# Second feed-forward product from rounded high and low parts, and the normed tile written in two halves

## The reference, cut to what matters

```python
a  = softmax over l of (x x^T), times x                   # self-attention, 2 x 2048 x 128
b  = weighted values (correlation, small ODE step, proj)  # one later stage
ffn = 2 layers, each:
    h = shift_token(x);  q, k, v = split(h @ wqkv)        # 8 heads of 64
    q = l2norm(q) * qs;  k = l2norm(k) * ksc
    q, k = q*cos*s + rotate_half(q)*sin*s, k*cos/s + rotate_half(k)*sin/s
    x = x + local_attention(8*q, k, v) @ wo               # windows of 64, own and past
    h = layernorm(shift_token(x)) * lg + lb
    a, g = split(h @ w1 + b1)                             # 2 x 341 columns
    x = x + (a * gelu(g)) @ w2 + b2
```

## Time and profile before

| what | value |
|---|---|
| median of three runs | 1556.6 us |
| the profiled execution | 1558.34 us |
| its span, first to last instruction | 1556.5 us |
| mean granted TensorE clock | 0.978 |
| PE, weight loads | 1438.8 us (92%), 1118.7 us (72%) |
| DVE, ACT, POOL | 1290.2 (83%), 1237.4 (79%), 895.0 us (57%) |

### The profile page before, as it was taken

One profiled execution on the slowest core, in us unless ns is written; L12 is line 12 of the kernel. 1 busy time (PEld: TensorE's weight loads), 2 busy tenths in 40 slices (PEclk: granted clock), 3 DMA queues, 4 the chain that ended last, 5 costly groups with the idle time before them and its releaser, 6 DMA issues.

```text
span 1556.5 us, 46462 instructions
## 1 busy us (share of the span) xinstructions
PE 1438.8 (92%) x18975; PEld 1118.7 (72%) x18975; DVE 1290.2 (83%) x1692; ACT 1237.4 (79%) x1834; POOL 895.0 (57%) x626
## 2 busy tenths in 40 slices
PE   5999997899999999999998757899999999999998
PEld 3777874777777777777776554677777777777776
DVE  6778758888899888988985866889899998988984
ACT  4886867688888888888885757788888888888884
POOL 4333105576666666776762545676666666666761
PEclk9999999999999999999999878999999999999999
DMA  4312003576676666757550003666667566675562
GB/s 115 112 51 85 18 5 75 121 131 120 121 129 127 118 122 127 125 119 127 115 107 18 0 5 69 134 126 120 121 129 125 118 126 124 124 124 121 115 111 67
DMA packets 359855, 157.46 MB, mean 101 GB/s; under 512 B 299410, under 2 KB 335836, under 8 KB 359644
## 3 DMA queue, kind: packets, MB, share of 16 engines
q1 hardware_dynamic: 359644, 154.51, 49.7%
HBM read 27.29 MB, written 6.29 MB: 22 GB/s over the span
## 4 chain that ended last, share of the span: by engine, by line
PE 58%; DVE 20%; issue 6%; ACT 5%; SPq 5%; DMA 4%; POOL 2%; DVEq 0%; POOLq 0%; ACTq 0%
PE PS L199 8%; PE PS L201 7%; PE PS L200 7%; PE PS L852 6%; PE PS L914 5%; PE PS L871 5%; DMA t<-t 3%; PE PS L827 3%; PE PS L834 3%; DVE t L1276 3%; DVE t L1283 2%; DVE t L1259 2%; DVE t L1266 2%; PE PS L860 2%; SPq L706 2%
## 5 line engine op out<-in xcount | busy, mean ns | idle before, releaser
L1444 POOL TENSOR_TENSOR t<-t 128x512 f32<-128x512 f32 x256 | 321.1, 1275 | 189.7 <-DVE t L1276 189.4
L1438 POOL TENSOR_TENSOR t<-t 128x1024 f32<-128x1024 f32 x128 | 309.0, 2414 | 164.5 <-DVE t L1266 164.4
L1276 DVE TENSOR_TENSOR t<-t 128x1024 f32<-128x1024 f32 x128 | 206.9, 1617 | 0.1
L199 PE MATMUL PS<-wqh,HH 128*128 128x512 f32 x384 | 178.0, 464 | 15.8 <-DVE t L1266 9.5
L1259 DVE TENSOR_REDUCE t<-t 128x16 f32<-128x1024 f32 x128 | 154.7, 1209 | 31.4 <-ACT t L1059 31.4
L1295 DVE TENSOR_REDUCE t<-PS 128x8 bf16<-128x1024 f32 x128 | 156.1, 1219 | 20.4 <-PE PS L801 20.4
L1059 ACT ACTIVATE t<-PS 128x1024 f32<-128x1024 f32 x128 | 131.6, 1028 | 49.2 <-PE PS L201 49.1
L1283 DVE TENSOR_TENSOR t<-t,PS 128x1024 bf16<-128x1024 f32 x128 | 155.1, 1212 | 7.9 <-ACT PS L1079 7.7
L1093 ACT ACTIVATE t<-PS 128x1024 f32<-128x1024 f32 x128 | 131.6, 1028 | 36.0 <-PE PS L834 32.4
L1072 ACT CAST t<-t 128x1024 bf16<-128x1024 f32 x128 | 133.8, 1046 | 27.6 <-POOL t L1444 26.9
L1266 DVE SCALAR_TENSOR_TENSOR t<-t,PS 128x1024 f32<-128x1024 f32 x128 | 154.9, 1210 | 0.6 <-ACT t L1066 0.6
(11 more groups left out here) (242 smaller groups left out, 3400.9 us busy)
## 6 DMA issues: line engine op xcount, KB each, us to landing
t<-t SPq DMA_DIRECT2D x254, 130.0 KB, 2.4
t<-turns SPq DMA_DIRECT2D x128, 128.0 KB, 2.9
t<-yT SPq DMA_DIRECT2D x108, 128.0 KB
t<-t SPq DMA_TRANSPOSE x304, 3.4
t<-in_c_rope SPq DMA_DIRECT2D x32, 128.0 KB, 2.2
turns<-t SPq DMA_DIRECT2D x32, 128.0 KB, 2.1
t<-in_L_attn_a_x SPq DMA_DIRECT2D x4, 512.0 KB, 7.1
t<-yT SPq DMA_DIRECT2D x16, 127.8 KB
```

Source lines behind the costliest of these rows:

```text
L199: e.matmul(o, ah, bh, start=not more, stop=False, skip_group_check=True)
L1276: e.e.tensor_tensor(BL.ta[i % 2].rearrange("p (x h) d -> p x h d", x=2), BL.qn.rearrange("p (x h) d -> p x h d", x=2), cos.to_broadcast([1 ...
L1438: e.e.tensor_tensor(BL.tc.rearrange("p (x h) d -> p x h d", x=2), BL.qn.rearrange("p (x h) d -> p x h d", x=2), sin.to_broadcast([128, 2, ...
L1444: e.e.tensor_tensor(tv[:, :, 32 * s:32 * s + 32], tv[:, :, 32 * s:32 * s + 32], BL.tc[:, :, 32 * (1 - s):32 * (1 - s) + 32], ALU.add).then ...
```

## The change

What it does, in three parts:

1. `w2` is kept as `w2h` and `w2l` (fp32r). Its six DMAs move from the end of SP's load to the middle of self-attention, into the buffer `BS.stage`; ACT makes the high parts at t = 18 and 22 of self-attention, POOL the low parts behind `scale_turns(1)`.
2. The hidden chunk is split as well: ACT casts (`high_hidden`) and POOL subtracts (`low_hidden`), one of the three parts in each of the steps r = 14, 15 and 16. `second` runs nine fp32r matmuls (`halves`) on these instead of three fp32 ones. `BL.hf` has two buffers instead of three, and `gated` now waits for `ff_lo` (the low part is made) instead of `ff_m2`. Behind the last step the parts are made on ACT, POOL and, for the last two half chunks, DVE.
3. DVE's `normed` is two instructions (q, then k) with a semaphore each (`la_q0`, `la_qn`); PE's `project` waits for either half by itself; POOL's sine product is two instructions too, and POOL's `rope` is split into `sine` and `turned_sums`, with `low_hidden` between them.

```diff
         def product(p, i):
+            if p == NC - 2 and i == 2:
+                return BL.o.rearrange("p b h d -> p (b h d)")[0:CW[i], :]
             if p < NC - 1:
-                return BL.hf[i][0:CW[i], :]
+                return BL.hf[(p + i) % 2][0:CW[i], :]
...
+        def hidden(t, p, i):
+            if p < NC - 1:
+                return t[0:CW[i], 1, i * CH:(i + 1) * CH]
+            return t[0:CW[i], i // 2, (1, 3, 3)[i] * CH:((1, 3, 3)[i] + 1) * CH][:, cols(p)]
...
-                e.wait_ge(S.la_qn, hi(i))
-                for x in range(2):
+                for x, read in enumerate((S.la_q0, S.la_qn)):
+                    e.wait_ge(read, hi(i))
                     xs = slice(x * 512, (x + 1) * 512)
                     mm = halves(e.e, PS[:, x, :], h, hl, wqh[:, l, xs], wql[:, l, xs])
...
             def second(C, bank):
                 l = layer_of(C)
-                e.wait_ge(S.ld_w2, 16 * 6)
+                e.wait_ge(S.w_2l, 2)
                 for i in range(3):
-                    e.wait_ge(S.ff_hf, 3 * (NP * u + C) + i + 1)
-                    mm = e.e.matmul(PS[:, bank, wide(C)], w2[0:CW[i], l, i, :], product(C, i), start=i == 0, stop=i == 2)
+                    e.wait_ge(S.ff_lo, 3 * (NP * u + C) + i + 1)
+                    wd = slice(0, CW[i])
+                    mm = halves(e.e, PS[:, bank, wide(C)], w2h[wd, l, i, :], w2l[wd, l, i, :], hidden(HH, C, i), hidden(HL, C, i),
+                                more=i > 0, stop=i == 2)
...
+            def high_hidden(C, i):
+                n = 3 * (NP * u + C) + i
+                e.wait_ge(S.ff_hf, n + 1)
+                e.wait_ge(S.ff_m2, NP * u + min(C, NC - 2))
+                e.e.copy(hidden(HH, C, i), product(C, i)).then_inc(S.ff_hi, 1)
...
                 if on(3):
                     exps(s - 3)
+                for i in range(3):
+                    if chunk_at(s, 14 + i) is not None:
+                        high_hidden(chunk_at(s, 14 + i), i)
                 behind_gelus = chunk_at(s, 13) is not None
                 if on(0) and not behind_gelus:
                     squares(s)
...
+            high_hidden(NC - 3, 2)
             deviation(Z0, 1)
...
             e.e.preload_act_table_set("natural_log_exp_and_others")
+            high_hidden(B, 0)
+            high_hidden(B, 1)
             deviation(Z1, 7)
...
-                e.e.scalar_tensor_tensor(BL.qn, ss[:, 16:32].rearrange("p (a o) -> p a o", o=1)
-                                         .to_broadcast([128, 2 * NH, DH]), 1e12,
-                                         PS[:, 0:2, :].rearrange("p x (h d) -> p (x h) d", d=DH), ALU.min,
-                                         ALU.mult).then_inc(S.la_qn, 1)
+                for x, done in enumerate((S.la_q0, S.la_qn)):
+                    hs = slice(NH * x, NH * x + NH)
+                    e.e.scalar_tensor_tensor(BL.qn[:, hs, :], ss[:, 16 + NH * x:16 + NH * x + NH].rearrange("p (a o) -> p a o", o=1)
+                                             .to_broadcast([128, NH, DH]), 1e12,
+                                             PS[:, x, :].rearrange("p (h d) -> p h d", d=DH), ALU.min,
+                                             ALU.mult).then_inc(done, 1)
...
-                if C < NC - 1:
-                    e.wait_ge(S.ff_m2, NP * u + C)
+                if C < NC - 2 or C == NC - 2 and i < 2:
+                    e.wait_ge(S.ff_lo, n - 2 + 1)
...
-            def rope(i):
+            def sine(i):
                 g = hi(i)
-                e.wait_ge(S.la_qn, g + 1)
+                e.wait_ge(S.la_q0, g + 1)
...
-                e.e.tensor_tensor(BL.tc.rearrange("p (x h) d -> p x h d", x=2), BL.qn.rearrange("p (x h) d -> p x h d", x=2),
-                                  sin.to_broadcast([128, 2, NH, DH]), ALU.mult).then_inc(S.la_tc, 1)
+                e.e.tensor_tensor(BL.tc[:, 0:NH, :], BL.qn[:, 0:NH, :], sin[:, 0].to_broadcast([128, NH, DH]), ALU.mult)
+                e.wait_ge(S.la_qn, g + 1)
+                e.e.tensor_tensor(BL.tc[:, NH:2 * NH, :], BL.qn[:, NH:2 * NH, :], sin[:, 1].to_broadcast([128, NH, DH]),
+                                  ALU.mult).then_inc(S.la_tc, 1)
+
+            def turned_sums(i):
+                g = hi(i)
                 e.wait_ge(S.la_ta, g + 1)
...
+            def low_hidden(C, i):
+                e.wait_ge(S.ff_hi, 3 * (NP * u + C) + i + 1)
+                e.e.tensor_tensor(hidden(HL, C, i), product(C, i), hidden(HH, C, i).bitcast(F32),
+                                  ALU.subtract).then_inc(S.ff_lo, 1)
...
                 if 0 <= s - 1 < TS:
-                    rope(s - 1)
+                    sine(s - 1)
+                for i in range(3):
+                    if chunk_at(s, 14 + i) is not None:
+                        low_hidden(chunk_at(s, 14 + i), i)
+                if 0 <= s - 1 < TS:
+                    turned_sums(s - 1)
```

More of the change, by code:

```diff
@@ L141, in build @@
                            tb=[arena(sc, [4 * DH]) for _ in range(4)], ysl=arena(sc, [CH]), ysf=arena(sc, [CH]),
-                           hf=[arena(sc, [CH]) for _ in range(3)])
+                           hf=[arena(sc, [CH]) for _ in range(2)])
                 rows4 = lambda ap: ap.rearrange("p a b c -> p (a b c)")
@@ L439, in self_attention_sp, with raw_w2 @@
                 e.wait_ge(S.ld_attw, 32 * (l + 1))
+            e.wait_ge(S.w_lo, 2)
+            for l in range(2):
+                for i in range(3):
+                    e.e.dma_start(raw_w2(l)[0:CW[i], i, :], a["L0_ffn_w2"][l, C0[i]:C0[i] + CW[i], :]).then_inc(S.ld_w2, 16)
             layer_turns(1)
             e.wait_ge(S.tr_st, 16 * 2 * NT)
+        def raw_w2(l):
+            return BS.stage[:, 384 * l:384 * l + 384].rearrange("p (i d) -> p i d", d=D)
         def self_attention_pe(e, stage):
@@ L567, in self_attention_pool @@
             scale_turns(1)
+            for l in range(2):
+                e.wait_ge(S.w_2h, l + 1)
+                e.e.tensor_tensor(w2l[:, l, 0:2, :], raw_w2(l)[0:114, 0:2, :], w2h[:, l, 0:2, :].bitcast(F32), ALU.subtract)
+                e.e.tensor_tensor(w2l[0:CW[2], l, 2, :], raw_w2(l)[0:CW[2], 2, :], w2h[0:CW[2], l, 2, :].bitcast(F32),
+                                  ALU.subtract).then_inc(S.w_2l, 1)
             plain_pool(e, x1, 1, (0, 2))
@@ L1224, in layers_act @@
                 gelu_there(Z0, i, bank)
+            high_hidden(B, 2)
             for i, bank in enumerate((1, 6, 3)):
                 gelu_there(Z1, i, bank)
+            for i in range(3):
+                high_hidden(Z0, i)
+            for i in range(3):
+                high_hidden(Z1, i)
             if u == 0:
@@ L1394, in layers_dve, with low_hidden @@
                     result(3, 1)
+            def low_hidden(p, i):
+                e.wait_ge(S.ff_lo, 3 * (NP * u + NC - 1))
+                e.wait_ge(S.ff_hi, 3 * (NP * u + p) + i + 1)
+                e.e.tensor_tensor(hidden(HL, p, i), product(p, i), hidden(HH, p, i).bitcast(F32),
+                                  ALU.subtract).then_inc(S.ff_lo, 1)
             def split_normed(p):
@@ L1418, in layers_dve @@
                 gated(Z1, i, bank)
+            for i in range(3):
+                low_hidden(Z0, i)
             add_second(B, 4)
+            for i in range(3):
+                low_hidden(Z1, i)
             add_second(Z0, 7)
@@ L1486, in layers_pool @@
                     low_for_feed_forward(NC - 1)
+            low_hidden(NC - 3, 2)
             add_residual(NC - 2)
             add_residual(NC - 1)
+            for i in range(3):
+                low_hidden(NC - 2, i)
             if u == 0:
```

22 lines of the change are left out of this document (13 added, 9 removed).

## The result

| kernel | median us (runs) | ratio to before, 95% interval |
|---|---|---|
| before | 1556.6 (1553.2 to 1558.4, and one run of 2313.9; 7) | |
| changed | 1563.5 (1560.28 to 1570.02, 7) | 1.0046 [1.0027, 1.0065] |
| changed, once more | 1561.2 (1555.5 to 1570.6, 12) | 1.0025 [1.0008, 1.0043] |

The account below looks back on a forecast made before the run. PE was taken to bound the kernel, with hardly a gap per settled period. Settled part +3, early start -3, ends +0.5 and self-attention nothing made +0.5 us on 1558.3; expected median 1557, case range 1549 to 1566, overall 1533 to 1578.

Parts of the forecast that it names:

- The main case: Settled periods: PE's 0.56 us gain is used up by waiting for late ACT; expected median 1557 us, chance 0.47.
- The two signs named for it: ACT's `copy_result` releases PE in steps of remainder 3 and 0; `normed` starts in remainder 3 8.0-8.4 us behind remainder 2.
- The second product: On PE, nine fp32r matmuls take 2.06 us instead of 2.62, 0.56 us less in each period.
- The chain in the step of remainder 2: From `normed` through sine, cosine, `low_hidden` and sums to ACT: `high` 0.6 us later, `exps` and `copy_result` 0.35 later.
- the "0.34": DVE's cosine product in the step of remainder 2 was to end 0.34 us earlier, at 4.36 behind `normed`.
- The lock: DVE's cosine and POOL's `low_hidden` exclude each other; DVE, issued at 3.17 before the sine's end at 3.28, goes first.
- rows 8: Trace rows before the change where a waiting DVE subtraction ran between two queued POOL instructions, taking 1.75 us.
- The rival in which POOL wins: `low_hidden` runs before DVE's cosine: +0.55 to +0.8 us per settled period, 1572 to 1579 us, chance 0.25.
- Per period: Each of 27 settled four-step periods becomes 0.1 us longer, between -0.1 and +0.35; together +3 us (-3 to +9).
- PE's gain comes through: Rival: the sums chain has slack, so settled periods lose 0.56 to 0.9 us; 1541 to 1533 us, chance 0.28.
- The early start, -3: `project` and the sine start earlier, helping in a stage's first 10 or so steps: -3 us (-7 to 0).
- The ends, +0.5: Added casts and subtractions against shorter products at both stage ends: last addition 0.2 us later per stage, +0.5 (-1 to +2).

Follow-up runs that it names:

- the halves alone: The kernel before plus only `normed` and the sine in halves, q's product waiting for the first half; second product unchanged: 1551.8 us, ratio 0.9962.
- the ends in the old form: The changed kernel with each stage's last whole chunk and two half chunks using three fp32 products, without casts or subtractions: 1559.8 us, ratio 1.0008.
- the fastest one: The changed kernel with early casts and subtractions, one subtraction behind the attention's low part, and residual additions moved: 1544.1 us, ratio 0.9910.
- early parts: The changed kernel with ACT's casts behind the rnorms one step earlier and POOL's subtractions moved off the settled chain: 1554.1 us, ratio 0.9975.
- early parts and tail: The changed kernel with early casts and subtractions, early residual additions, and the last whole chunk's casts behind the half piece's gelus: 1556.0 us, ratio 0.9992.

## Why the prediction was right, and where not

- *The main case is the one that happened:* PE's gain used up by the wait ahead of it. The two signs named for it are in the trace: ACT's `copy_result` is the releaser of PE in the steps of remainder 3 and 0 (0.23 at 587.75; the weight load at 596.17), and `normed` starts 8.07 us apart there (forecast 8.0 to 8.4) in the first two thirds of a stage. In the last third it is 8.3 to 8.7, which the forecast did not have.
- *The second product:* 2.06 forecast, 2.18 measured; the nine start 0.23 apart, the first 0.33 ahead of its successor.
- *The chain in the step of remainder 2*, from `normed`: sine's end 3.28 forecast, 3.30 measured; cosine issued at 3.17, measured 3.16, and done at 4.36, measured 4.38 (0.39 earlier than before; the "0.34" took the 0.07 of the split off twice); `high` 8.16 and 8.04; `exps` 10.3 and 10.1; `copy_result` ending at 13.3 and 13.1. PE's product into bank 7 was to be 0.3 late; the step of remainder 3 became 0.43 longer.
- *The lock:* DVE won, as rows 8 had it. `low_hidden` at 2.29 and 2.24 us is the subtraction held up by the cosine. The rival in which POOL wins has no instance in the settled part; the margin of 0.1 us held in both traces.
- *Per period:* forecast +0.1; measured 35.71 against 35.72, made of +0.43, -0.23, +0.11 and -0.31. Over 27 periods +3 was forecast, and the two middles gave +1.2 and -0.1.
- *PE's gain comes through* did not happen, and its price was somewhat high: with the subtraction all but cut out the kernel ran at 1544.9 (forecast for that case: 1541 to 1533), 13 under the kernel before and not 15 to 24, of which the halves alone give 6. In that trace the step of remainder 1 gave 0.28 us back in every period, and the ends cost 3.3 us more than before.
- *The early start, -3:* in the changed kernel nothing of it can be seen by itself; the first 8 steps took 68.2 and 65.1 us against 67.8 and 65.1. Alone it gives 6 us, most of it in the settled part of the second stage, where I had given it nothing because it "runs into the same late `exps`". That was right for the combination only. There the halves are worth 10 to 13 us (ratio 1.0111 without them), since they are what lets the cosine go ahead of `low_hidden` so early. I had priced this in the chain, not as a term.
- *The ends, +0.5, is the mis-sized term:* they measured +6.2 us in the profiled execution and +4.0 in the second, both outside -1 to +2. The casts ahead of the last deviation, which the forecast had (1.0 us), measured 1.0. Three things were left out. ACT's cast ahead of `copy_result` behind the last maxima is 0.5 us at each end. POOL's residual additions now run beside DVE's cast and subtraction (0.71 us alone, 2.83 and 1.69 in the two profiles, of which 0.3 to 1.0 reaches the end). And PE's granted clock fell to 0.95 in three of the four ends, 1.5 us each. The shorter products at the ends give 0.6 to 1.0 us of this back. Of the +0.8 per end that remains with the ends in the old form, 0.5 is that first cast.
- *Sum:* 1557 forecast, 1563.5 and 1561.2 measured. By the terms the difference is the ends (+6.2 and +4.0 for +0.5) and the early start (0 for -3), against a settled part of +1 for +3 and, in the two profiles, 2.1 us less between the stages, which the forecast did not have. So some of the nearness of the sum is misses that cancel. That the ends are what the medians show is only in part tested: undoing their casts gave 3 to 6 us in the changed kernel and nothing in the fastest one.

## What to carry to other kernels

A shorter product gains only what the engines level with it can give back: ask which engine releases the instruction ahead of it, and where that one's new work stands in its own queue. Put added casts and subtractions into the waits that the profile shows on that engine, not beside the operation to which they belong; here the same work, moved by some rows, went from 0.25 to 0.46% slower to 0.7% faster, and with the residual additions moved as well to 0.9%. Then follow what stands behind the new place too: one exchanged pair of POOL rows (ahead of or behind the attention's low part) was worth 0.5 us in one step and, after the next step gave some back, 0.3 in every period. Ends of stages need a sum of their own, with the granted clock in it.

## What the runs showed of the hardware that was not expected

- A DVE cast of 128x256 to fp32r, with one input in SBUF, took 1.43 and 0.97 us beside POOL instructions and 0.29 alone: in these traces it is held up as an instruction with two inputs is.
- A POOL subtraction of a single column (114x1) took 1.18 us while the cosine ran (first row DVE, then POOL), and 0.18 to 0.20 us in the steps of remainder 0, where no cosine stood in its way. So cutting its columns took 1.1 us off it and left the wait for the cosine:

```profile
572.14 1.22 DVE L1318 TENSOR_TENSOR t<-t 128x1024 f32<-128x1024 f32 x1
572.23 1.18 POOL L1526 TENSOR_TENSOR HL<-t,HH 114x1 fp32r<-114x1 f32 x1
573.43 2.51 POOL L1501 TENSOR_TENSOR t<-t 128x512 f32<-128x512 f32 x2
```

- The granted clock after one and the same wait differs. In the first end PE waits 2.3 us for DVE in the changed kernel and with early parts; then products of 256 columns started 0.21 us apart in the one (the lower level, 1.2 GHz, for some 3 us; 0.95 over the stretch) and 0.12 in the other (1.00). The first row is the changed kernel's, the second that with early parts:

```profile
846.86 0.53 PE L200 MATMUL PS<-HH,w1h 128*114 128x256 f32 x1 [2.32 <-DVE HL L1448]
```

```profile
844.08 0.34 PE L200 MATMUL PS<-HH,w1h 128*114 128x256 f32 x1 [2.31 <-DVE HL L1447]
```

Of the 20 ends of the ten traces (the changed kernel twice) whose end pieces have casts and subtractions, 12 were at 0.95; of the 8 ends of the four traces without them, none. In ten of the 12 the stretch of the lower level began behind that wait of PE (2.3 us, or 1.9 at the second end); in the first ends of the kernels with the residual additions moved and with early parts and tail it began earlier, at 830.7 and 829.1. What tips it in a given run stays open.
